# Steps of the expert gate moved to other tile slots inside an attention kernel

## What is computed

```python
q = rope(elu(q) + 1); k = rope(elu(k) + 1)
attn_out = softmax(q @ k.T * scale) @ v
x = x + layernorm(attn_out + lepe(v))          # lepe: 3-tap convolution along the sequence
xt = layernorm(x)
scores = softmax(xt @ gate_w.T)                 # 8 experts
idx = top_k(scores + gate_b, 2)                 # the two chosen experts of each token
x = x + layernorm(sum of the two chosen experts, weighted by their scores, + shared expert)
```

## Time and profile before

| | |
|---|---|
| median of 3 runs | 1266.2 us (1265.22 to 1266.6) |
| the profiled execution | 1265.12 us, its span 1263.3 us |
| DVE busy in the span | 1071.7 us (85%) |
| PE busy | 1059.5 us (84%) |
| ACT busy | 937.9 us (74%) |
| POOL busy | 833.7 us (66%) |
| attention phase, by DVE's row maxima | 48.5 to 847 us |

### The profile page before, as it was taken

One profiled execution on the slowest core, in us unless ns is written; L12 is line 12 of the kernel. 1 busy time (PEld: TensorE's weight loads), 2 busy tenths in 40 slices (PEclk: granted clock), 3 DMA queues, 4 the chain that ended last, 5 costly groups with the idle time before them and its releaser, 6 DMA issues. The chain is left out here.

```text
span 1263.3 us, 21973 instructions
## 1 busy us (share of the span) xinstructions
PE 1059.5 (84%) x6376; PEld 445.4 (35%) x6376; DVE 1071.7 (85%) x2451; ACT 937.9 (74%) x1782; POOL 833.7 (66%) x1087
## 2 busy tenths in 40 slices
PE   1498989999999999999998999898799999887810
PEld 0012222222322222222222222222578778655600
DVE  2398899999999999999999999991687889999944
ACT  1117888888888878788788788889699898867712
POOL 5445466676578787888778878645364546776475
PEclk9559999999999999999999999999799999999965
DMA  2453332422423334234233242203134544454412
GB/s 67 116 133 122 97 87 65 107 83 74 115 69 111 90 99 115 79 102 120 68 103 104 78 110 84 73 19 111 51 100 137 192 157 156 129 152 132 120 51 80
DMA packets 108982, 128.20 MB, mean 101 GB/s; under 512 B 14224, under 2 KB 81844, under 8 KB 108596
## 3 DMA queue, kind: packets, MB, share of 16 engines
q1 hardware_dynamic: 98848, 105.94, 29.5%
q0 software_dynamic: 8192, 16.79, 4.7%
q10 hardware_dynamic: 1824, 4.06, 0.9%
HBM read 58.85 MB, written 59.51 MB: 94 GB/s over the span
## 5 line engine op out<-in xcount | busy, mean ns | idle before, releaser
L1075 DVE TENSOR_REDUCE MX<-psS 128x1 f32<-128x512 f32 x1024 | 647.0, 679 | 64.8 <-PE psS L762 63.0
L974 ACT ACTIVATE PR<-psST 128x512 f32<-128x512 f32 x986 | 535.9, 600 | 127.3 <-PE psST L750 125.2
L762 PE MATMUL psS<-KS,QS 48*128 48x512 bf16 x1024 | 371.3, 400 | 40.8 <-DMA KS<-scratch_parts 23.8
L750 PE MATMUL psST<-QS,KS 51*128 51x512 bf16 x986 | 337.6, 385 | 42.3 <-ACT PR L974 25.8
L776 PE MATMUL psPV<-PR,V 128*32 128x512 f32 x2048 | 274.3, 608 | 5.8 <-ACT PR L974 1.0
L750 PEld LDWEIGHTS psST<-QS,KS 51*128 51x128 bf16 x986 | 78.5, 93 | 398.9 <-ACT PR L974 370.0
L1968 POOL DMA_INDIRECT SHARED<-scratch_y,FROM x128 | 130.2, 1017 | 51.6 <-issue 37.9
L465 POOL DMA_INDIRECT scratch_x<-XN,POSI x128 | 128.6, 1005 | 36.3 <-issue 34.0
L762 PEld LDWEIGHTS psS<-KS,QS 48*128 48x128 bf16 x1024 | 87.8, 93 | 105.5 <-DVE MX L1075 73.5
L1533 PE MATMUL psY<-WD,HA 128*128 (+1 forms) x496 | 67.7, 279 | 13.3 <-issue 6.9
L1507 PE MATMUL psH<-XH,WS 128*128 128x512 f32 x169 | 74.0, 438 | 2.9 <-DVE XL L1720 2.0
(11 more groups left out here) (217 smaller groups left out, 1845.7 us busy)
## 6 DMA issues: line engine op xcount, KB each, us to landing
scratch_parts<-PT SPq DMA_DIRECT2D x192, 128.0 KB, 2.4
QS<-scratch_parts SPq DMA_DIRECT2D x64, 192.0 KB, 3.3
KS<-scratch_parts SPq DMA_DIRECT2D x64, 192.0 KB, 4.2
XR<-scratch_x SPq DMA_DIRECT2D x46, 256.0 KB, 2.8
scratch_y<-YR SPq DMA_DIRECT2D x46, 256.0 KB, 2.0
RES<-EL SPq DMA_DIRECT2D x64, 128.0 KB, 2.0
scratch_x<-ZERO SPq DMA_DIRECT2D x18, 256.0 KB
X<-in_x SPq DMA_DIRECT2D x16, 256.0 KB, 4.7
```

What stands on the lines that cost most here:

```text
L750: nc.tensor.matmul(bank(st_banks(t), k)[:], KS[t.par][rows, h // 2, kc * P:(kc + 1) * P], QS[t.par][rows, h // 2, :], start=True, stop=Tru ...
L762: nc.tensor.matmul(bank(psS, k)[:], QS[b.par][rows, h // 2, qc * P:(qc + 1) * P], KS[b.par][rows, h // 2, :], start=True, stop=True).then_ ...
L974: nc.scalar.activation(PR[:, s % 2, HEAD_AT[j], :], bank(st_banks(t), k)[:], ACT.Exp, scale=SCALE).then_inc(st_exp, 1)
L1075: nc.vector.tensor_reduce(out=MX[:, qc, h:h + 1], in_=bank(psS, k)[:], axis=AX.X, op=ALU.max).then_inc(s_max, 1)
```

## The change

The change touches four things. Nothing is added or removed: every instruction of before is there after, in another place.

1. `GATE_AT`: steps 2 to 4 and 7 to 14 stand at other places. Steps 15 to 21 stay.
2. `RANK_AT`: steps 24, 25 and 26 move from (1, 2), (1, 3), (2, 0) to (2, 0), (2, 2), (3, 0).
3. ACT takes the exponential of the gate (L239) at the end of slot 2 and not of slot 3.
4. POOL computes the gate's scores before the first four scatters of the iteration and not behind them.

```diff
-                if s == 3 and p is not None:
+                if s == 2 and p is not None:
                     ends.exponentials(act, p)
...
-            GATE_AT = {(1, 2): 1, (1, 3): 2, (4, 2): 3, (4, 3): 4, (6, 2): 7, (6, 3): 8, (7, 2): 9, (7, 3): 10, (8, 2): 11,
-                       (8, 3): 12, (9, 2): 13, (9, 3): 14, (10, 2): 15, (10, 3): 16, (12, 0): 17, (12, 1): 18, (12, 2): 19,
+            GATE_AT = {(1, 2): 1, (2, 0): 2, (3, 1): 3, (3, 2): 4, (4, 2): 7, (4, 3): 8, (5, 0): 9, (5, 2): 10, (6, 0): 11,
+                       (9, 2): 12, (9, 3): 13, (10, 0): 14, (10, 2): 15, (10, 3): 16, (12, 0): 17, (12, 1): 18, (12, 2): 19,
...
-            RANK_AT = {(0, 1): 22, (0, 2): 23, (1, 2): 24, (1, 3): 25, (2, 0): 26}
+            RANK_AT = {(0, 1): 22, (0, 2): 23, (2, 0): 24, (2, 2): 25, (3, 0): 26}
...
+                if paired(t) is not None:
+                    ends.gate_scores(pool, paired(t))
                 if out.live:
                     ends.scatter(pool, out, 0)
-                if paired(t) is not None:
-                    ends.gate_scores(pool, paired(t))
```

## The result

The changed kernel takes 1287.7 us (median of 4 runs, 1287.54 to 1290.97) against 1266.35 us for the kernel before (1265.22 to 1266.6): a ratio of 1.0173, with a 95% interval of 1.016 to 1.0185. The forecast was 1270.0, its range ended at 1272.5. The profiled execution took 1287.67 us, its span is 1285.9 us against 1263.3.

A forecast was written before the change was run, and what follows sets the result against it. The prediction took DVE to bound gate iterations. Terms 4 x 0.76 + 1.1 + 0.3 - 0.16 + 0 gave + 4.3 us, hence 1269.4 or 1270.5 from 1265.1 or 1266.2; forecast 1270.0, range 1264.5 to 1272.5 us.

The forecast's parts named there:

- What bounds the kernel, and what holds a step: DVE bounds gate iterations; a small two-SBUF-tensor step waits until a running wide POOL instruction ends, 2.9 us in iteration 8.
- Step 11, L346, to (6, 0): At (6, 0): requested at 515.68, held to the end of the second L1170, next maximum at 516.66, 0.83 us lost.
- Slots 6 to 9: Thirteen maxima and L271 in slots 6 to 9, none held, plus 0.7 us of waits: (9, 2) at 525.75.
- Step 2, L331: At (2, 0): old hold goes, but L331 is held by L1144 until 501.99; next maximum 0.1 us later.
- the rival: At (2, 0): L331 gets in before L1144, margin 0.04 us; sum - 0.3, 1265 to 1266 us; chance 0.19.
- Scores before scatters: On POOL: 0.65 us of scores move ahead of four scatters; same sum, L1170 stays at about 514.1, no new waits.
- Steps 7 to 10: At (4, 2) to (5, 2): beside scatters, not held; holds of 0.72 and 0.71 go, 4 x 0.13 comes before (6, 0).
- L348: Step 12 at (9, 2): requested at 526.35 after both L1182 are over; its hold of 0.80 us goes.
- L340 and L342 of slot 10: At (10, 0) and (10, 2): both held beside L1185, taking 0.8 and 1.0 us; iteration ends 0.76 later.
- Iteration 4: No scatters, so the rotary chain starts 2.4 us earlier over steps 8, 9 and 11: holds 3.4 against 2.5, + 1.1.
- Ranks: L386 at (2, 0) loses 0.44 instead of 0.65 inside L1144: - 0.16 over four iterations, + 0.3 in iteration 5.

The follow-up runs named there:

- f2_stop: Kernel with all small two-tensor steps clear of wide POOL work, plus two unread row maxima at (6, 0) of iterations 6, 8, 10, 12: 1355.39 us, kernel before 1356.61.
- f5_stop: Kernel with all small two-tensor steps clear of wide POOL work, plus five unread row maxima at (6, 0) of iterations 6, 8, 10, 12: 1377.06 us, ratio 1.0159.
- a2_gap_first: Changed kernel plus a POOL wait that opens a gap between the two L1170: 1268.06 us, ratio 1.0021 to the kernel before.
- d2_scores_first: Kernel before with only POOL's gate scores moved ahead of the four scatters: 1365.95 us against 1356.61, ratio 1.0097.
- a0: The changed kernel itself, run again on another chip as the measure for others: 1290.65 us, ratio 1.0185 to the kernel before.
- a1_onehot_away: Changed kernel with L344 and L346 moved to (5, 1) and (5, 2), before the rotary products: 1268.22 us, ratio 1.0008 to the kernel before.
- e2: Changed kernel plus a POOL wait ahead of L1173, opening a gap behind the second L1170: 1365.2 us in one run; kernel before 1352.5 us.

## Why the prediction was wrong, step by step

**What bounds the kernel, and what holds a step: right, and misread in one point.** DVE's time was the iteration's, and wide POOL instructions hold two-tensor steps. But the rule was put as "held until a wide POOL instruction, if one is running, ends". The rows allowed another reading that I did not see. In the earlier trace rows L1170, L1170 and L1173 follow without a space (514.06 + 2.53 = 516.59 against 516.55), and the L340 of the earlier trace rows was requested in the last of the three, which the first gap follows. Its 0.93 us could not tell the end of an instruction from the start of a gap. Of the rows named, only L348, let in between two L1182, spoke for the end of the instruction.

**Step 11, L346, to (6, 0): this is the step that failed.** I put "free (0.15) and held to the end (0.97)" as the bounds and took 1.0 us, to the end of the second L1170, though even by my own timing the wide work ran on behind it. Measured: 2.97, to the gap behind L1173. An upper bound by the next gap in POOL's row would have been 2.2 us by my own timing, from the request at 515.68 to about 517.9; at the place where the request really fell, in the first L1170, 2.97. That is 2.0 us of the 4.1 by which iteration 8 missed the forecast.

**Slots 6 to 9: the second miss.** I put 0.7 us of waits for PE, from a row at the full clock. Measured: 2.9, since PE's clock was low behind its stop at L346. That is 2.2 us; the two make 4.2, and the other terms came out 0.1 better. The prediction has no sentence on what a stop of DVE does to PE's clock. f2_stop and f5_stop show that a stop of PE at this place is enough, with no hold on POOL in it.

**Step 2, L331: the rival came true.** It was requested at 507.19, 0.05 us before L1144 at 507.24, took 0.22, and L1144 took 0.65 and not 0.61. But what the rival then promised, - 0.3 us in all, did not come, by the same failed step: L1170 starts 20.1 us after the iteration and not 19.8 (the first L465 now stands 0.40 us for the scores), so L346 falls 0.42 before the end of the first L1170, and there is no gap behind it to slip into. It was a matter of less than 0.1 us: in a2_gap_first L331 was requested 0.03 behind the start of L1144 and held for 0.65.

**Scores before scatters: right in this kernel, not by itself.** In the changed kernel, step 4 is done early and POOL waits for nothing but those 0.40 us. d2_scores_first shows how the early steps 3 and 4 carry it: without them the rotary chain is 2.9 us late (iteration 12), and a 4.1 us hold is the result.

**Steps 7 to 10, L348, L340 and L342 of slot 10: right.** L340 and L342 of slots 4 and 5 take 0.22 beside the scatters, L348 0.21, and those of slot 10 take 0.56 to 0.83 and 0.98 against 0.8 and 1.0 forecast, each within a L1185.

**Iteration 4: right in size.** + 1.14 against + 1.1, with holds of 0.43, 0.70, 0.56, 0.83 and 0.99 us at the five places named, and 0.51 at L331. In part this is luck: in a0, the same kernel, the clock fell in iteration 4 too, and it lasted 55.3 us, 3.3 more than before.

**Ranks: right for L386, wrong by 0.1 for the iteration.** L386 takes 0.57 to 0.58 beside L1144 and the rank iterations 7, 9 and 11 last 49.71, 0.1 more than before where I had 0.04 less; iteration 5 is + 0.47 against + 0.3. After, iteration 9, answering to the earlier trace rows:

```profile
564.26 0.58 DVE L386 TENSOR_TENSOR SHARED<-OH,CAND 128x128 f32<-128x128 bf16 x1
```

```profile
564.08 0.61 POOL L1144 TENSOR_SCALAR EXQ<-EXQ 128x512 f32<-128x512 f32 x1 [1.14 <-ACT EXQ L906]
```

**The sum.** Without the hold of L346 the change is worth what the other terms gave: a2_gap_first is at + 1.7 us (0.06 to 0.36%) and a1_onehot_away at + 1.9 (not clear of noise) against their kernel before; in a1's trace iterations 6 to 12 give back 0.5 us each and iteration 4, with its fall of the clock, takes 3.0. So the direction was right for the wrong reason in the main: the forecast had + 0.76 in each of the four iterations from a hold in slot 10, and the step that makes the kernel slower is L346. The size was off by a factor of five, by one term of four copies and the clock behind it. The range failed because its upper end took the hold's bound from the length of one instruction.

A page of the Trainium skill gives the same rule as my prediction. SBUF — State Buffer, section Summary: rules for kernel authors, says that of a DVE instruction with two SBUF inputs and a GpSimd instruction that reads SBUF, the second to issue blocks until the first finishes. By that rule L346 in the changed kernel would end with the first L1170, after some 0.5 us; the trace shows 2.97, and the measurement decides.

## What to carry to other kernels

Price a small two-tensor DVE step near wide POOL work by the distance to the next real gap in POOL's row, not by what is left of the instruction that runs, and place it in a gap, beside scatters (but not in the last one before a wide chain: d2_scores_first, 4.06 us), or just before POOL starts after standing idle. Where POOL's work comes in a chain without gaps, one wait on its own semaphore makes one, at some 0.1 us. And before a stop of DVE is priced, ask what PE does then: where it stops PE too, the time at half clock behind it can cost more than the stop.

## What the runs showed of the hardware

- But for the cases of the next point, a hold ended with POOL's first gap. Boundaries without a gap did not let a step in when it was requested in the first L1170 (2.97, 2.96, and 1.36 with a gap behind the second), in the second one (1.96), or at the end of the scatter before them (4.06). Gaps of some 0.1 us did.
- Exceptions stay open. In iteration 4 of the changed kernel, L340 was requested at 307.06, in an L1170 of 306.11 to 307.41, and took 0.43 us, although L1173 starts at 307.35: it got in at a boundary without a visible gap. L348 in the earlier trace rows also got in between the two L1182 (though each of these waits for a conversion on ACT, and so may leave a gap that the recorded ends hide), and so did L348 in a1, which ended at 529.52 although the L1185 behind the two L1182 is recorded from 529.45. What makes such a boundary open is not settled.
- A step that is requested 0.05 us before a POOL instruction, behind a gap, isn't held, and the POOL instruction takes 0.04 us more: L331 and L1144, in iterations 6 to 12. Requested 0.03 us behind the start (a2), it is held to the end. Requested 0.26 us before the start, but inside a scatter (d2), it is held too.
- PE's granted clock fell to 0.5 behind stops of 0.90 (e2), 1.40 (f2), 2.82 (after) and 3.19 us (f5) in slots 5 to 7, and in iteration 4 of a1 behind three stops of at most 0.60. It did not fall behind a stop of 1.03 us in iteration 13 of f2_stop. In iteration 4 the changed kernel had stops of 0.46, 0.33, 0.47, 0.19 and 0.41 us in one trace (after) and the same within 0.01 in another (a0); the clock stayed at 1.00 in the first and fell for 6.8 us in the second, at the price of 2.1 us. So the length of the last stop does not decide alone, and what does was not tested further.
